# Products of ones between TensorE's work in the last four steps of a two-layer sequence kernel

## The reference, cut to what matters

```python
x = x + _L1_attn_ref(_layernorm(x), w_in, conv_w, conv_b, w_B, w_C, w_out)
x = x + _L1_ffn_ref(_layernorm(x), w_gate, w_up, w_down)

def _L1_attn_ref(x, ...):              # a gated state-space layer
    xp, z = jnp.split(x @ w_in, 2, axis=-1)
    xc = silu(depthwise_conv(xp, conv_w, taps=4) + conv_b)
    h = h * 0.9 + 0.1 * (xt @ w_B)     # scan over the 256 tokens
    ys = h @ w_C
    return (ys * silu(z)) @ w_out

def _L1_ffn_ref(x, ...):               # all operands rounded to FP4 by blocks of 16
    gate = fp4_linear(x, w_gate)
    y = fp4_linear(x, w_up)
    return fp4_linear(silu(gate) * y, w_down)
```

## Time and profile before

| | us |
|---|---|
| median of three runs | 609.23 |
| the runs | 608.47, 609.23, 613.55 |
| profiled execution, its own time | 605.77 |
| its span in the trace | 604.0 |
| granted TensorE clock, mean over the span | 0.973 |
| TensorE busy in the span | 542.9 (90%) |

### The profile page before, as it was taken

The page is one execution under the profiler, slowest core; times in us unless marked ns, Lnnn a source line. Parts: engine busy times, 40 slices in busy tenths (PEclk is TensorE's granted clock), DMA queues, the critical chain, the costliest instruction groups (busy, mean ns, idle before and its releaser), DMA issues. The chain is left out here.

```text
span 604.0 us, 15157 instructions
## 1 busy us (share of the span) xinstructions
PE 542.9 (90%) x4517; PEld 444.8 (74%) x4518; DVE 447.0 (74%) x1179; ACT 316.2 (52%) x899; POOL 339.1 (56%) x514
## 2 busy tenths in 40 slices
PE   1799999999999898988999997998999999999966
PEld 1567667766777577788998986787788777887754
DVE  2689999899888549943457543478999999998873
ACT  2355766666666554415565652345545564556432
POOL 5468777777776622247567105556666775763231
PEclk9999999999999999998999998998999999999975
DMA  7000100110010155012522211100111111110000
GB/s 210 24 20 29 46 28 27 43 35 26 35 43 27 56 167 139 1 27 61 146 69 56 40 36 30 18 10 9 24 31 18 17 22 30 17 17 9 10 19 17
DMA packets 35193, 25.55 MB, mean 42 GB/s; under 512 B 4752, under 2 KB 31568, under 8 KB 35152
## 3 DMA queue, kind: packets, MB, share of 16 engines
q1 hardware_dynamic: 29264, 20.32, 11.5%
q0 software_dynamic: 5888, 4.72, 5.1%
HBM read 14.09 MB, written 6.75 MB: 34 GB/s over the span
## 5 line engine op out<-in xcount | busy, mean ns | idle before, releaser
L1149 PE MATMUL a_ps_a<-a_qx,a_kt 32*128 32x512 f32 x512 | 69.1, 628 | 1.0 <-DMA a_qx<-a_qs 1.0
L1712 POOL DMA_INDIRECT x<-yg_dram,pos x32 | 55.9, 1747 | 11.6 <-issue 11.6
L1316 POOL TENSOR_TENSOR d_hq<-d_fh_v,d_fh_scale 128x352 f32<-128x352 f32 x32 | 27.9, 888 | 61.3 <-DVE d_fh_v L1342 61.3
L442 POOL TENSOR_SCALAR_AFFINE_SELECT a_at<-a_at 128x512 f32<-128x512 f32 x80 | 50.5, 650 | 14.6 <-ACT a_at L523 14.6
L199 POOL DMA_INDIRECT rows<-xn_dram,slot_token x40 | 40.1, 1003 | 25.3 <-ACT c_rows L1478 11.0
L523 ACT ACTIVATE a_at<-a_ps_a 128x512 f32<-128x512 f32 x80 | 44.5, 600 | 11.6 <-PE a_ps_a L1149 10.0
L1521 DVE TENSOR_TENSOR c_hid<-c_act,c_ps 128x352 f32<-128x352 f32 x39 | 20.2, 518 | 36.4 <-ACT c_act L1464 36.4
L1149 PEld LDWEIGHTS a_ps_a<-a_qx,a_kt 32*128 32x128 f32 x512 | 31.7, 188 | 16.9 <-issue 16.3
L207 PE MATMUL d_ps_A<-d_xnT,wmix 128*128 128x256 f32 x128 | 37.1, 290 | 0.6 <-ACT d_silu L1794 0.6
L715 DVE TENSOR_TENSOR a_at<-a_ps_a,mask 128x512 f32<-128x512 f32 x48 | 32.8, 684 | 6.4 <-PE a_ps_a L1149 5.2
L208 PE MATMUL d_ps_A<-d_xnT,wmix 128*128 128x256 f32 x128 | 36.1, 282 | 0.0
(11 more groups left out here) (347 smaller groups left out, 1758.3 us busy)
## 6 DMA issues: line engine op xcount, KB each, us to landing
a_qx<-a_qs SPq DMA_DIRECT2D x64, 64.0 KB, 1.9
a_at<-in_L_ffn_w_eDF_dram SPq DMA_DIRECT2D x16, 176.0 KB, 3.2
yg_dram<-c_y SPq DMA_DIRECT2D x19, 128.0 KB, 1.8
xn_dram<-a_xn2s SPq DMA_DIRECT2D x16, 128.0 KB, 1.9
out_dram<-x SPq DMA_DIRECT2D x16, 128.0 KB, 1.9
w<-in_L_ffn_w_eFD_dram SPq DMA_DIRECT2D x2, 512.0 KB, 5.7
x<-in_L_attn_x_dram SPq DMA_DIRECT2D x1, 768.0 KB, 5.4
rows<-xn_dram,slot_token POOLq DMA_INDIRECT x40, 2.8
```

The source lines that it names most:

```text
L442: nc.gpsimd.affine_select(at[:, t, r, :, :], at[:, t, r, :, :], pattern=[[0, 4], [1, P]], compare_op=ALU.is_ge, fill=0.0, base=0, channel_ ...
L1149: last = nc.tensor.matmul(ps_a[:, r, :, :], kt[rows, b.par, c_, tile(t)], qx[rows, b.par, :, c_, tile(t)], start=(c_ == 0), stop=(c_ == 1))
L1712: nc.gpsimd.indirect_dma_start(out=x[:, t, :], out_offset=None, in_=g["yg_dram"][:, :], in_offset=bass.IndirectOffsetOnAxis(ap=g["pos"][:, ...
```

## The change

TensorE's stream gets a helper that issues n products of the tile of ones with itself into the first 128 columns of `ps_M`, and calls it in five places of the written-out steps:

- after the down product of step 13: a wait on `s_x4`, then 12 products;
- after the transposes of `xq` of batch 15 in step 14: 3;
- ahead of the down product of step 14, behind its waits: 3;
- after the down product of step 14: 10;
- ahead of the down product of step 15, behind its waits: 3.

```diff
+            def keep_busy(n):
+
+                for _ in range(n):
+                    nc.tensor.matmul(ps_M[:, 0:P], g["ones"][:, :], g["ones"][:, :], start=True, stop=True)
+
@@ body, after the transposes of xq
                     last.then_inc(s_xqp, 1)
+                    if c.m is None and c.off == B - 1:
+                        keep_busy(3)
@@ body, the down product
                     wait(pe, s_h, c, per=2)
                     if not live(c):
                         wait(pe, s_x5, d, ago=1)
+                    if d.m is None and d.off >= B - 2:
+                        keep_busy(3)
                     for t in range(2):
...
                     last.then_inc(s_f, 1)
+                if d.m is None and d.off == B - 3:
+                    pe.wait_ge(s_x4, B)
+                    keep_busy(12)
+                if d.m is None and d.off == B - 2:
+                    keep_busy(10)
```

## The result

The changed kernel takes 608.12 us (median of 22 runs, 606.05 to 611.38), the kernel before, run beside it, 610.74 us (22 runs, 608.47 to 614.22). The ratio is 0.9944, 95% interval 0.9929 to 0.9958: 3.4 us of 610.7. The two medians alone differ by 2.62 us (0.9957), at the edge of that interval. The forecast was 0.9945.

What follows compares the result with a forecast made beforehand. Bound: TensorE on the path at 1.2 GHz from 581.2 to the end. Keeping the clock high moved the end from 601.31 to 597.97, gain 3.34 us including 0.80 of bare products; 605.9 us on the median, range 602.2 to 610.5.

Steps and rivals of the forecast that it cites:

- 1.: After step 13's down product: twelve products end at 583.03, hidden before xq at 583.72, with 0.69 us of cover.
- 2.: Step 14: gate products start at 585.03 instead of 585.34; the three products are hidden with 0.13 us to spare.
- 3.: Step 14: gate and up products take 2.17 us; silu starts at 587.24 instead of 589.26, 2.02 earlier.
- 4.: Step 14, VectorE: the addition's 0.42 us wait goes; it starts at about 591.71 instead of 594.11, 2.40 earlier.
- 5.: After step 14's down product: ten products end at 593.70, when transposes could start; no cover, cost taken as 0.
- 6.: Step 15: second transposes to down product take 1.13 us instead of 1.54; work ready at 595.57.
- step 7: Step 15: three bare products add 0.80 us; down product takes 1.60 instead of 2.93; end 597.97 instead of 601.31.
- the bound 611.7: All fills: products at 0.488 us despite a high clock make the end 2.47 us slower, 611.7 on the median.
- Rival 1: Step 15: six transposes count as waiting, clock falls again; only 1.34 us faster, 607.9 on the median; chance 0.08.
- Rival 2: Steps 14 and 15: clock falls anyway, fills delay real work; 7.15 us slower, 616.4 on the median; chance 0.06.
- rival 3: All fills, the ten first: products cost more than the down product's row; 611.7 us on the median; chance 0.04.
- Rival 4: Step 14: VectorE's rounding, 3.94 us, hides the clock's gain; already in the sum, no chance of its own.

Runs made afterwards that it cites:

- e2: Changed kernel without the three products ahead of each of the last two down products; tail 20.85 us, ratio 0.9942 to the kernel before.
- e8: Changed kernel with 30 products in place of 10 after step 14's down product; tail 25.04 us, one execution of 613.45 us, no ratio.
- e1: Changed kernel with only the twelve products after step 13 kept, the other four fills removed; tail 23.91 us, ratio 0.9975 to the kernel before.
- e3: Changed kernel without the twelve products after step 13, the other four fills kept; tail 22.98 us, ratio 0.9989 to the kernel before.
- e4: Changed kernel with 20, 4, 4, 16 and 4 transposes in place of its five fills of products; tail 22.78 us, ratio 0.9961 to the kernel before.
- e10: Changed kernel with transposes as fills: 32, 6 and 28 for 12, 3 and 10 products, none ahead of down products; tail 20.87 us, ratio 0.9898.
- e5: Kernel before with products of ones in three earlier waits (seven, eight, six), none in the last steps; tail 24.97 us, ratio 1.0019.

## Why the prediction was right

By its steps, with times of the changed trace moved back by 6.11 us so that they stand on the scale of the prediction:

1. The twelve products hidden: yes, with more cover than 0.69 us. They began 0.16 earlier, at 579.67, and took 2.84 instead of 3.20, and 1.21 us of wait is left.
2. Gate products at 585.03: 585.10. The three products hidden, with 0.26 to spare.
3. Silu 2.02 us earlier, at 587.24: it starts at 587.33, 1.93 earlier, and the hid product behind it at 587.83 instead of 589.75. The gate and up products took 2.20, said 2.17.
4. The addition's wait gone: yes, it starts at 591.68; said 591.71. Two small errors cancel here: silu was 0.09 less early than said, and the addition starts 0.08 before the rounding's step in front of it ends, where I had counted from that end.
5. The ten products with no cover left: too careful. The transposes wait 0.44 us behind them, since ten took 2.40 and not 2.67, and began at 590.83 and not 591.03. The three ahead of step 14's down product took 0.77. The cost of 0 that I took holds.
6. Work for the last down product ready at 595.57: 595.59.
7. The last three products bare on the path: yes. The last down product began 0.77 us later than it could have, said 0.80; what they cost in all is 0.68 (e2).

Sum: 3.45 us in the trace, 3.34 said; ratio 0.9944, 0.9945 said. So near a hit of the ratio is partly luck, as its interval is 0.9929 to 0.9958. In time the forecast was 605.9 and the median is 608.12: of these 2.2 us, 1.5 are the kernel before, which took 610.74 beside it and not 609.23. The 0.11 us that the trace has beyond the sum lie in step 7: from the work being ready to the addition's start it took 2.31 us (595.59 to 597.90) and not 2.44. The price of a product of ones was the term too large. I took the length of the row of the down product over six, 0.267, which holds the end of its last instruction; neighbours overlap, and the spacing of starts is what a longer row costs. By it a product of ones costs 0.223 (e8), and a call of the down product behind other work as much: 595.60 to 596.94 for six. Most products are hidden, so the error hardly showed.

The range is not what its sentence says: 605.1 less 3.5 is 601.6 and not 602.2, and the upper end, 610.5, lies below the bound 611.7 that it names.

That it is the clock, e1, e3 and e4 show: where the clock was low for a part of the tail, that part's operations had the low prices of the earlier trace rows and the tail was longer by them.

**Rival 1** (the clock falls again in step 15 as transposes do not count): did not happen, and e10 shows its premise wrong. **Rival 2** (the fills run at the low clock in front of real work, 7.15 slower): did not happen, and its price was wrong. e3, with the clock low ahead of the later fills, is the nearest case, and it was 2.0 us faster than before in the tail. What this rival had wrong is "low to the end": in e3 the clock came back while TensorE worked without a pause, and the later fills then ran at 1.00. The case of the slower side that is real is a fill longer than its wait (e8, +3.5 us against the changed kernel), which the prediction had only as dearer products (rival 3). **Rival 4**, that VectorE's rounding caps the gain, is right: from hid's start at 593.94 to the end of L1341 at 597.87 it is 3.93 us, 3.94 before.

One argument of the prediction was weaker than it sounded: that waits under 1.6 us do not bring a fall. In e1 two waits of 1.21 and 0.93 us close together did. Nor was it so that all waits left are at most half of what stood before a fall: the one ahead of the transposes of xq is 1.21 us, three quarters of 1.58, because twelve products are shorter than I had said. The clock held all the same. By e1, the three products in the wait behind those transposes had a part in that, which I had put down to filling a short wait. So the clock stayed as was said, though part of the argument for it had failed: that much is luck.

## What to carry to other kernels

Where TensorE's work at the very end of a program waits on others, look at the granted clock of those last microseconds beside the mean: 22.8 us at half clock hid behind a mean of 0.973. Work without a result is worth adding only inside a wait that is on the chain to the end; size it by its own measured price to end just before the wait does, and put none directly ahead of real work that is ready. What raising the clock is worth elsewhere has to be measured: in e5 no gain was seen. When an effect is a few us and executions scatter by six, measure from a shared instruction close to the change in one trace, and let the times only confirm. Take more than one trace where the clock may fall in some executions and not in others.

## What the runs showed of the hardware that was not expected

- The low clock came back within the gate products of step 14 when three products of ones joined them to the transposes before (e3, back before 593.8), and did not in the same products of the kernel before with a 0.93 us wait ahead. Behind the same wait it did come back in e1, before 595.4.
- The same wait of 2.0 us was followed by half clock in one execution (until 273.66, kernel before) and by full clock in another (until 273.74, changed kernel).
- Transposes of 32-bit 128x128 tiles hold the clock as products do (e10), at 0.11 us each in a row (32 in 3.66 us, 20 in 2.35 in e4: 1.31 for 12 more).
- A product of ones with itself into one place has a spacing of 0.223 us in a long row (e8), the same as the down product's behind other work (1.34 us for six calls): in these rows, writing the same place again and again costs nothing extra.
- Taking away some 5 us of time at half clock far from the end (e5, by the mean clocks of the timed executions) gave no gain that the times could show (1.0019, 0.9996 to 1.0041).
